# A cross-attention and mixture-of-experts kernel: another opening order, and down products three slots behind their expert

## The reference

```python
x = x + xattn(layernorm(x), ctx)                # 8 x 256 x 128
x = x + ffn(layernorm(x))

def xattn(q, k):
    query, key_p, value = q @ Wq.T, k @ Wk.T, k @ Wv.T
    sim = einsum('bqd,bkd->bqk', query, key_p)
    sim = (sim - mean(sim, (1, 2))) * rsqrt(var(sim, (1, 2)) + EPS)   # per batch
    return softmax(sim) @ value @ Wo.T

def ffn(x):
    shared = swiglu(x @ sw1 + sb1) @ sw2 + sb2
    p = softmax(x @ gate_w + gate_b)             # 8 experts
    cw = p where p is one of the token's two largest, else 0
    routed = sum over e of cw[e] * (swiglu(x @ rw1[e] + rb1[e]) @ rw2[e] + rb2[e])
    return shared + routed
# swiglu(h): a, b = split(h, 2); silu(a) * b ; FFN width 128
```

## Time and profile before

| | |
|---|---|
| time, median of 3 runs | 137.28 us (136.94 to 137.58) |
| the profiled execution | 138.01 us, of which span 135.9 us |
| PE | 128.9 us busy (95%), 627 instructions |
| PEld | 96.5 us (71%) |
| DVE | 108.5 us (80%), 312 |
| ACT | 83.1 us (61%), 161 |
| POOL | 22.8 us (17%), 40 |

### The profile page before, as it was taken

How to read it: one execution, slowest core, us unless ns; L and a number is a source line. 1 busy time by engine, 2 the same in 40 slices (tenths; PEclk the granted TensorE clock), 3 DMA queues, 4 the chain that set the end, 5 groups by cost and what they waited for, 6 DMA issues and landing times.

```text
span 135.9 us, 2098 instructions
## 1 busy us (share of the span) xinstructions
PE 128.9 (95%) x627; PEld 96.5 (71%) x627; DVE 108.5 (80%) x312; ACT 83.1 (61%) x161; POOL 22.8 (17%) x40
## 2 busy tenths in 40 slices
PE   7998998998999999999999899999899999999992
PEld 7775787757776766788678576787458776778862
DVE  1458998777999999879969999639979894899872
ACT  1546869895637459964665269954382785655340
POOL 7142632156260020500400020000400000000000
PEclk9999999999999999999999999999999999999999
DMA  4997400002900000059000002089000023930022
GB/s 117 321 352 206 142 5 2 0 2 83 353 36 0 0 0 2 5 209 384 24 5 0 0 0 77 5 229 391 5 0 2 0 77 116 376 130 0 5 77 77
DMA packets 8828, 12.97 MB, mean 95 GB/s; under 512 B 1321, under 2 KB 6994, under 8 KB 8306
## 3 DMA queue, kind: packets, MB, share of 16 engines
q1 hardware_dynamic: 8242, 12.62, 26.7%
q10 hardware_dynamic: 576, 0.23, 0.7%
HBM read 11.73 MB, written 1.11 MB: 94 GB/s over the span
## 4 chain that ended last, share of the span: by engine, by line
issue 42%; PE 32%; POOL 8%; DVE 6%; ACT 5%; DMA 3%; POOLq 1%; DVEq 0%
PE bank L947 27%; POOL row_powers L379 3%; POOL w_rest L403 3%; DMA cw_all<-cw_dram 2%; POOL ln_rstd L388 2%; PE bank L963 1%; DVE act L830 1%; DMA cw_dram<-cw_rows 1%; POOLq L51 1%; POOL sim_r L394 1%; DVE silu L822 1%; ACT xn L509 1%; DVE act_rest L839 1%; PE bank L1009 1%; DVE x L851 1%
## 5 line engine op out<-in xcount | busy, mean ns | idle before, releaser
L555 ACT ACTIVATE silu<-bank,b_cols 128x512 f32<-128x512 f32 (+1 forms) x37 | 24.9, 676 | 25.1 <-PE bank L947 24.7
L947 PE MATMUL bank<-x_head,w_head 128*128 128x512 f32 x72 | 35.2, 488 | 0.4 <-DVE act L830 0.4
L830 DVE SCALAR_TENSOR_TENSOR act<-bank,b_cols,silu 128x512 f32<-128x512 f32 (+1 forms) x37 | 27.1, 735 | 2.7 <-ACT silu L555 1.7
L947 PE MATMUL bank<-x_head,w_rest 128*128 128x512 f32 x72 | 28.4, 395 | 0.0
L947 PE MATMUL bank<-x_rest,w_head 128*128 128x512 f32 x72 | 28.2, 392 | 0.0
L822 DVE TENSOR_TENSOR silu<-silu,cw_all 128x512 f32<-128x512 f32 (+1 forms) x31 | 20.6, 668 | 4.2 <-DMA cw_all<-cw_dram 2.3
L947 PE MATMUL bank<-act,w_sb 128*128 128x512 f32 x44 | 22.5, 592 | 0.0
L947 PEld LDWEIGHTS bank<-x_head,w_head 128*128 128x128 f32 x72 | 13.6, 189 | 5.8 <-issue 2.6
L947 PEld LDWEIGHTS bank<-x_rest,w_head 128*128 128x128 f32 x72 | 13.6, 189 | 4.6 <-issue 2.9
L947 PEld LDWEIGHTS bank<-x_head,w_rest 128*128 128x128 f32 x72 | 13.5, 188 | 3.1
L839 DVE TENSOR_TENSOR act_rest<-act,act_head 128x512 fp32r<-128x512 f32 x12 | 8.3, 690 | 3.3 <-ACT act_head L547 2.8
(11 more groups left out here) (130 smaller groups left out, 212.9 us busy)
## 6 DMA issues: line engine op xcount, KB each, us to landing
cw_all<-cw_dram SPq DMA_DIRECT2D x4, 1024.0 KB, 6.9
cw_all<-cw_dram SPq DMA_DIRECT2D x4, 512.0 KB, 4.9
cw_all<-cw_dram SPq DMA_DIRECT2D x6, 256.0 KB, 3.7
x_sb<-in_x_dram SPq DMA_DIRECT2D x4, 256.0 KB, 3.9
w_sb<-in_L_ffn_rw_dram SPq DMA_DIRECT2D x1, 1024.0 KB, 7.6
ctx_sb<-in_ctx_dram SPq DMA_DIRECT2D x4, 192.0 KB, 4.0
out_dram<-x SPq DMA_DIRECT2D x3, 256.0 KB, 2.2
w_sb<-in_L_ffn_rw_dram SPq DMA_DIRECT2D x1, 512.0 KB, 7.0
```

Of the source, the lines that this page charges most:

```text
L555: scalar.activation(silu[:, k, cols], hid(n, 0)[:, cols], ACT.Silu, bias=b1_cols[:, 0, e:e + 1]).then_inc(silu_sb, 1)
L830: dve.scalar_tensor_tensor(act[:, k, cols], hid(n, 1)[:, cols], b1_cols[:, 1, e:e + 1], silu[:, k, cols], ALU.add, ALU.mult).then_inc(act_ ...
L947: return pe.matmul(dst, lhs, rhs, start=start, stop=stop, skip_group_check=True)
```

## The change

1. The opening is in another order on four engines. `first_statistics(1)` on DVE and `first_rstd(1)` on POOL come right behind those of chunk 0; `ln_veps` has a third row so that the two don't wait for each other. On PE, `transpose_x(1)` comes ahead of `project_u(1)`, which is in two halves; the scores of both batches of chunk 1 come ahead of the transposes of the first softmax, and `scores_average(1)` right behind the attention of chunk 0. On ACT the four exponentials are no longer interleaved with the copies of `prob_t`.
2. Group 1 of `w1` is divided by ACT (cast) and POOL (subtraction), as the other groups are.
3. `down(n - 3)` stands in slot n in place of `down(n - 2)`; `down(32)` and `down(33)` both stand between the two halves of slot 35. `out_bias` moves from e = 2 to e = 3. `act` has four buffers in place of three.
4. Divided are slots 8 to 11, 16 to 20 and 25 to 32, seventeen. Their heads and rests are made in slot m + 2, those of 9, 18 and 27 in slot m + 1, so that slots 10, 19 and 28 have two of each.

```diff
-        act = sb("act", [P, 3, N])
+        act = sb("act", [P, 4, N])
...
+        def u_groups(c):
+            return [[0], [1]] if c <= 1 else [[0, 1]]
...
-        DIVIDED = [n for n in range(NX, LAST - STRAIGHT) if n >= NX * (C - 1) or n % NX in (0, 3, 4)]
+        DOWN_BEHIND = 3
+        DIVIDED = [n for n in range(NX - 1, LAST - STRAIGHT) if n >= NX * (C - 1) or n % NX in (0, 1, 2, 7, 8)]
+
+        def divided_in(n):
+
+            return [m for m in (n - 2, n - 1) if m in DIVIDED and m == (n - 1 if m % NX == 0 else n - 2)]
...
             first_rstd(0)
+            first_rstd(1)
             scores_rstd(0)
-            first_rstd(1)
-            pool.wait_ge(w1_rest_sb[1], 1)
+            pool.wait_ge(negmax_sb, 1)
             gate_rests()
             w1_rests(0)
+            w1_rests(1)
             second_rstd(0, 0)
...
             v_copy(0)
+            x_copy(1)
             u_copy(1)
-            x_copy(1)
-            scalar.wait_ge(negmax_sb, 1)
-            exponential(0, 0, 0)
-            exponential(0, 0, 1).then_inc(prob_sb, 1)
-            exponential(0, 1, 0)
+            exponentials(0)
             prob_copy(0)
-            exponential(0, 1, 1).then_inc(prob_sb, 1)
             prob_copy(1)
+            scalar.wait_ge(rw1_in, 16)
+            w1_heads(1)
+            w1_heads(2)
             x_copy(2)
-            scalar.wait_ge(rw1_in, 16)
-            w1_heads(2)
             ctx_copy(2)
...
-                if e == 2 and c >= 1:
+                if e == DOWN_BEHIND and c >= 1:
                     out_bias(c - 1)
...
-                if n - 1 in DIVIDED:
-                    act_heads(n - 1)
+                for m in divided_in(n):
+                    act_heads(m)
...
             first_statistics(0)
+            first_statistics(1)
...
-            head, rest, whole = w1_parts(1)
-            dve.wait_ge(rw1_in, 16)
-            own(dve.tensor_copy(head, whole))
-            wait_own()
-            dve.tensor_tensor(rest, whole, head.bitcast(F32), ALU.subtract).then_inc(w1_rest_sb[1], 1)
...
-                if n - 1 in DIVIDED and e <= 1:
-                    act_rests(n - 1)
+                if e == 1:
+                    for m in divided_in(n):
+                        act_rests(m)
 
                 def between():
-                    if n - 1 in DIVIDED and e >= 2:
-                        act_rests(n - 1)
+                    if e != 1:
+                        for m in divided_in(n):
+                            act_rests(m)
...
                 if n == LAST:
+                    down(n - 3)
                     down(n - 2)
...
-                if 2 <= n < LAST:
-                    down(n - 2)
+                if DOWN_BEHIND <= n < LAST:
+                    down(n - DOWN_BEHIND)
```

More of the change, by code:

```diff
@@ L93, in xattn_moe_kernel @@
         ln_mv = sb("ln_mv", [P, 2, TC, 2])
-        ln_veps = sb("ln_veps", [P, 2, TC])
+        ln_veps = sb("ln_veps", [P, 3, TC])
         ln_rstd, ln_shift = sb("ln_rstd", [P, TC]), sb("ln_shift", [P, TC])
@@ L224, in batch_cols, with u_count @@
             return slice(S * js[0], S * (js[-1] + 1))
+        def u_groups(c):
+            return [[0], [1]] if c <= 1 else [[0, 1]]
+        def u_count(c, j):
+            return CB * c + j + 1 if c <= 1 else c + CB + 1
         def u_bank(c, g):
-            return bank[2] if c == 0 and g == 1 else early(c)[1]
+            return bank[2] if c <= 1 and g == 1 else early(c)[1]
         def late(c, g):
@@ L463, in u_copy @@
             def u_copy(c):
-                for g, js in enumerate(groups(c)):
-                    scalar.wait_ge(u_ps, upto(c, g))
+                for g, js in enumerate(u_groups(c)):
+                    scalar.wait_ge(u_ps, u_count(c, js[-1]))
                     if c >= 2:
@@ L546, in act_heads @@
                 scalar.wait_ge(act_sb, n + 1)
-                copy(act_head[:, n % 3, :], act[:, n % 3, :]).then_inc(act_head_sb, 1)
+                scalar.wait_ge(y_ps, n - 2)
+                copy(act_head[:, n % 3, :], act[:, n % 4, :]).then_inc(act_head_sb, 1)
             def expert_silu(c, e):
@@ L598, in _ @@
             x2_heads(0, 0)
+            first_chunk_normalise(range(IB + 1, TC))
+            v_copy(2)
+            x2_heads(0, 1)
             scalar.wait_ge(small_in, 16 * 3)
@@ L673, in ln_variance @@
                 wait_own()
-                if c >= 1:
-                    dve.wait_ge(ln_r[which], c if which == 0 else done(c - 1))
+                if which == 0 and c >= 2:
+                    dve.wait_ge(ln_r[0], c - 1)
+                elif which == 1 and c >= 1:
+                    dve.wait_ge(ln_r[1], done(c - 1))
                 t = slice(ts[0], ts[-1] + 1)
-                dve.tensor_scalar(ln_veps[:, which, t], ln_mv[:, which, t, 1], EPS, None, ALU.add).then_inc(ln_var[which], 1)
+                dve.tensor_scalar(ln_veps[:, which if which == 1 else 2 * (c % 2), t], ln_mv[:, which, t, 1], EPS, None, ALU.add).then_inc(ln_var[which], 1)
             def second_shift(c, g):
@@ L827, in expert_gate @@
                     dve.wait_ge(b_ps, n + 1)
-                    if n >= 3:
-                        dve.wait_ge(y_ps, n - 2)
-                    dve.scalar_tensor_tensor(act[:, k, cols], hid(n, 1)[:, cols], b1_cols[:, 1, e:e + 1], silu[:, k, cols],
+                    if n >= 4:
+                        dve.wait_ge(y_ps, n - 3)
+                    dve.scalar_tensor_tensor(act[:, n % 4, cols], hid(n, 1)[:, cols], b1_cols[:, 1, e:e + 1], silu[:, k, cols],
                                              ALU.add, ALU.mult).then_inc(act_sb, 1)
@@ L838, in act_rests @@
                 dve.wait_ge(act_head_sb, divided(n))
-                dve.tensor_tensor(act_rest[:, n % 3, :], act[:, n % 3, :], act_head[:, n % 3, :].bitcast(F32), ALU.subtract).then_inc(act_rest_sb, 1)
+                dve.tensor_tensor(act_rest[:, n % 3, :], act[:, n % 4, :], act_head[:, n % 3, :].bitcast(F32), ALU.subtract).then_inc(act_rest_sb, 1)
             def final(c):
@@ L885, in _ @@
             second_statistics(0, 1)
-            scores_moments(1)
+            scores_variance(1)
             second_shift(0, 1)
@@ L967, in project_u @@
                 pe.wait_ge(ctxt_sb, c + 1)
-                for g, js in enumerate(groups(c)):
+                if c == 1:
+                    pe.wait_ge(v_ready, 1)
+                for g, js in enumerate(u_groups(c)):
                     mm(u_bank(c, g)[:, batch_cols(js)], qk_t[:, :], ctx_t[:, c % 2, batch_cols(js)]).then_inc(u_ps, 1)
@@ L980, in batch_scores @@
             def batch_scores(c, j):
-                pe.wait_ge(u_ready, upto_batch(c, j) if c == 0 and j == 0 else done(c))
+                pe.wait_ge(u_ready, u_count(c, j))
                 for i in range(IB):
@@ L1115, in down @@
                     pe.wait_ge(act_sb, n + 1)
-                    mm(OUT_B[:, :], w2_sb[:, e, :], act[:, k, :], first, final).then_inc(y_ps, 1)
+                    mm(OUT_B[:, :], w2_sb[:, e, :], act[:, n % 4, :], first, final).then_inc(y_ps, 1)
             def to_tokens(c):
@@ L1141, in straight_down @@
                         tile = slice(i * P, (i + 1) * P)
-                        last = mm(TILE_BANKS[i][:, 0:D], act[:, n % 3, tile], w2_sb[:, n % NX, :], False, n == LAST)
+                        last = mm(TILE_BANKS[i][:, 0:D], act[:, n % 4, tile], w2_sb[:, n % NX, :], False, n == LAST)
                         if n == LAST:
@@ L1160, in _ @@
             pe.transpose(bank[0][:, 0:D], wo_sb[:, :], ident[:, :]).then_inc(setup_ps, 1)
-            scores(0)
+            pe.wait_ge(xt_sb, 1)
+            batch_scores(0, 0)
+            batch_scores(0, 1)
             pe.wait_ge(wv_in, 16)
@@ L1219, in _ @@
                 if n == 0:
-                    pe.wait_ge(u_ready, done(2))
+                    pe.wait_ge(u_ready, u_count(2, 1))
                     pe.wait_ge(v_ready, 3)
```

33 lines of the change are left out of this document (14 added, 19 removed).

## The result

| | before | after |
|---|---|---|
| time, median | 137.35 us (136.94 to 137.58, 4 runs) | 138.22 us (138.16 to 138.27, 4 runs) |
| ratio, with its 95% interval | 1 | 1.0061 (1.0034 to 1.0089) |
| the profiled execution | 138.01 us, span 135.9 us | 138.26 us, span 136.5 us |
| PE, DVE, ACT, POOL busy | 128.9, 108.5, 83.1, 22.8 us | 128.0, 110.3, 86.3, 23.9 us |

The change costs 0.9 us. In a second comparison it is 138.23 us against 137.39, a ratio of 1.007 (1.0047 to 1.0094). PE has 0.9 us less to do, as the five cheaper products make it, and the kernel is slower. The granted clock is 1.00 in both.

The account below looks back on a forecast made before the run. PE and DVE were taken to bound together, both full in slots 2 to 8. Terms -0.40 - 0.10 - 0.65 + 0.10 - 0.30 + 0.69 + 0.70 gave +0.04, say 0: 137.3 us, range 135.9 to 138.2.

Parts of the forecast that it names:

- likeliest case: Whole kernel: no change, 137.3 us, with bounds from 136.4 to 138.0; chance 0.45.
- (a): Whole kernel: PE bounds by its own sum, the expected waits are absent, gain 1.26, 136.0 us; chance 0.31.
- (b): Opening: POOL's subtraction of group 1 ends after 19.15 and delays ln_rstd, +0.75, 138.0 us; chance 0.19.
- three bounds: Limits on terms: opening -0.9 to +0.3, slots 9 to 17 -1.1 to -0.2, end +0.3 to +0.8.
- The opening, -0.40: Chunk 0's norm: DVE takes the attention result 0.37 earlier, leaving 0.4 us gained by the second transposes and router.
- Slots 2 to 8, -0.10: DVE's chain stays full, so PE arrives early and waits; gain 0.1 us, bounds 0 and -0.3.
- The 52.6: Start in us forecast for transpose_cw, the routing weights' transposes of chunk 1, where it was 53.01.
- Slots 9 to 17, -0.65: Wait near 77 goes and DVE loses slot 14's subtraction, against a new 0.3 wait for ctx_t; 0.65 us gained.
- Slots 18 to 34, +0.10 and -0.30: Slot 19's casts and subtractions end 0.1 behind cw_all; from slot 27 the 0.30 wait before 119.10 goes.
- Rival (c): Slots 10, 19, 28: pairs of casts and subtractions hold back the gate, up to 1.5 more, 138.7 us; chance 0.05.
- Slot 35, +0.69 and +0.70: The owed down product costs 0.69, and PE waits 0.70 for act(32)'s rest, queued on DVE behind final(2).

Follow-up runs that it names:

- second profile of the kernel before: Kernel before with only a fourth act buffer and a third ln_veps row, both unused: 137.65 us against 137.39, ratio 1.0013.
- old set three slots behind: Changed kernel with the earlier choice of divided products (three in each of chunks 1 and 2, none of slots 8, 26): 137.91 us, ratio 1.0033.
- the opening alone: Kernel before with the new order of the opening and group 1 of w1 divided, nothing of the slots changed: 137.35 us against 137.39, ratio 0.9993.

## Where the forecast held and where it failed

The forecast was no change, 137.3 us. The time is 138.22, slower by 0.6% and clear of noise (1.0034 to 1.0089), 0.9 us above the forecast and at the very end of the range (138.2). That it lies at the range's end and not beyond is luck. The likeliest case ended at 138.0; the range went on to take in the rivals (a) and (b), and neither of them is what happened. Nor did 136.4 to 138.0 follow from the three bounds beside it: taken all one way, they give about 136.0 to 138.5. By the stretches, against the second profile of the kernel before:

- **The opening, -0.40: held**, -0.31 (from the average to the transposes of the routing weights of chunk 0, 17.17 us for 17.48, the whole of it still there in slot 8). POOL's subtraction took the estimated 1.28 us, so rival (b) falls; the time near its 138.0 has another cause. The transposes of the second norm came at 20.90, as said (21.0), but 0.42 of that is the earlier start of the execution. The order gave 0.22 there and not 0.54.
- **Slots 2 to 8, -0.10: next to nothing, as it was**, 0.0. PE waits at 36.57 and 47.20, and the two engines still meet at the weights of chunk 1. The 52.6 that I named came out as 52.27, and with the 0.42 of the earlier start that is 52.69. Rival (a) is wrong here: PE's own sum does not bound.
- **Slots 9 to 17, -0.65: mis-sized**, -0.37 (-0.26 against the first profile). Its parts were as said: no wait near 77, a wait for `ctx_t` (0.58 between starts, 0.35 above a product). The old set three slots behind takes 25.09 us against 25.14, so that the distance lends nothing here, and the gain is that of the new set. I had let DVE's freed 0.6 count whole, because it seemed to agree with PE's sum. This is the largest part of what the sum missed.
- **Slots 18 to 34, +0.10 and -0.30: the sum held, the working did not**, -0.17 (-0.10 against the first profile). Split at the router of chunk 3 it is +0.47 and -0.64; against the first profile, which waited longer for `cw_all` in slot 19 and less in slot 28, -0.04 and -0.06. So the split can't be read from these profiles. The runs that change one thing can: beside the opening alone, the distance gives 0.57 and 0.53 here, and the new set then takes 0.79 back ahead of the router (24.14 for 23.35) and 0.03 behind it. I had given the distance nothing up to the router, and had written that the rest of act(19) makes PE late at the transposes of slot 22, "but there is room up to the router". Both were wrong, and nearly cancelled. I had looked at the pair in slot 19 and not at 19 and 20, one each in the slots 21 and 22; exchanging these two for 21 and 22 gives 0.50 back. Rival (c) had the kind of mechanism, queued subtractions that hold up the gate, with the wrong place, and 0.05. The router came at 101.18, 1.04 earlier than the earlier trace rows, as said (1.1), but 0.42 of that is again the earlier start.
- **Slot 35, +0.69 and +0.70: held**, +1.61. The owed product stands there. The rest of act(32) was there 2.54 us after the transposes began (126.35, and 128.20 with its 0.69), where I had added up 2.53. The wait measured 0.84 and, taken away, 0.9.

By these stretches -0.31, 0, -0.37, -0.17 and +1.61 give +0.76, where my terms gave +0.04. The 0.72 between them are 0.28 of slots 9 to 17, 0.22 of slot 35, 0.10 of slots 2 to 8, 0.09 of the opening and 0.03 of slots 18 to 34. By cause, each from the runs that differ by it alone: the opening -0.22, the third slot of distance +0.49, the new set +0.48. The last two, the slots, were forecast at +0.44 together; they cost 0.97 behind the new opening and 0.77 behind the old one.

In slot 4 DVE and POOL stand in each other's way as in the earlier trace rows; the first row is DVE's, the second POOL's:

```profile
37.18 1.59 DVE L699 SCALAR_TENSOR_TENSOR ln_shift<-ln_mv,ln_rstd 128x4 f32<-128x4 f32 x1
```

```profile
36.94 1.82 POOL L416 TENSOR_TENSOR w_rest<-w_sb,w_head 128x768 fp32r<-128x768 f32 x1
```

In the opening this cost nothing, since `ln_veps` was made at 18.79, behind POOL's 17.39 to 18.67. The rule that a DVE instruction with two SBUF inputs and a GpSimd one that reads SBUF shut each other out (the Trainium skill, SBUF — State Buffer, section Who interferes with whom) agrees with the 1.59 us; the instruction that I had taken to be exposed to it did not meet it.

## What to carry to other kernels

A product moved later by a slot is a loan. Look first at where it is paid back, and at what stands on the other engine's queue ahead of its operands there: here the loan was worth some 1.0 to 1.1 us and the return 1.6, of which 0.9 was one subtraction on the wrong side of another operation. When cheaper products need preparing on a second engine, choose them by what that engine has queued behind the preparation, not by their number: of two kernels with seventeen divided products, the one with two of them exchanged was 0.6 us faster. And before resting a margin of 0.5 us on one profiled execution, take a second, and see whether what a stretch loses by a longer wait for a DMA comes back in the next one.
